# A transformer layer on one core: another prologue order, the loop's pieces and VectorE's order rearranged

## The reference

```python
x = x + attention(layernorm(x))          # eps 1e-5
x = x + ffn(layernorm(x))

def attention(x):                        # 16 heads of 8
    q, k, v = (x @ Wq + bq), (x @ Wk + bk), (x @ Wv + bv)    # then by heads
    q, k, v = (head_layernorm(z, scale, bias) for z in (q, k, v))   # eps 1e-6, over the 8
    scores = einsum('bqhd,bkhd->bhqk', q, k) * 8 ** -0.5
    out = einsum('bhqk,bkhd->bqhd', softmax(scores), v)
    return out.reshape(b, s, 128) @ Wo + bo

def ffn(x):                              # w_gate, w_up (384, 128), w_down (128, 384): int32 / 127
    h = silu(x @ w_gate.T) * (x @ w_up.T)
    return h @ w_down.T
```

## Time and profile before

| | us |
|---|---|
| median of 3 runs | 330.37 (330.34 to 330.46) |
| the profiled execution | 330.57 |
| its span in the trace | 328.8 |
| busy: PE / ACT / DVE / POOL | 297.1 / 268.8 / 238.7 / 48.5 |

### The profile page before, as it was taken

One profiled execution on the slowest core, in us unless ns is written; L12 is line 12 of the kernel. 1 busy time (PEld: TensorE's weight loads), 2 busy tenths in 40 slices (PEclk: granted clock), 3 DMA queues, 4 the chain that ended last, 5 costly groups with the idle time before them and its releaser, 6 DMA issues.

```text
span 328.8 us, 10326 instructions
## 1 busy us (share of the span) xinstructions
PE 297.1 (90%) x4002; PEld 131.8 (40%) x4002; DVE 238.7 (73%) x631; ACT 268.8 (82%) x300; POOL 48.5 (15%) x93
## 2 busy tenths in 40 slices
PE   7877957899999999999999999999998998789996
PEld 7773311233243424352353325342432332222676
DVE  4998997358887797869786888689774856272365
ACT  4429949999989998889979998999889998999511
POOL 7610200041004100140004100410021010110020
PEclk9999989999999999999999999999999999999999
DMA  6534140210325023401422032302320243000000
GB/s 187 161 112 142 34 160 4 80 54 0 101 96 163 2 78 119 139 20 64 127 87 73 0 119 85 116 0 96 96 99 2 66 130 131 2 0 2 34 3 32
DMA packets 21716, 24.76 MB, mean 75 GB/s; under 512 B 2096, under 2 KB 17712, under 8 KB 21680
## 3 DMA queue, kind: packets, MB, share of 16 engines
q1 hardware_dynamic: 21104, 23.59, 22.7%
q10 hardware_dynamic: 576, 0.69, 0.7%
HBM read 15.36 MB, written 8.65 MB: 73 GB/s over the span
## 4 chain that ended last, share of the span: by engine, by line
PE 48%; ACT 26%; issue 13%; DVE 9%; DMA 2%; POOL 1%; ACTq 1%; SPq 0%; POOLq 0%; DVEq 0%
ACT probs L771 25%; PE oacc L912 19%; PE side L844 14%; PE scores L897 9%; PE side L837 3%; DMA y<-in_x 2%; DVE qk_c L1090 1%; PE scores L998 1%; DVE x2n L1074 1%; ACT th L737 1%; PE scores L798 1%; POOL rs L591 1%; PE side L998 1%; DVE stats L1065 0%; DVE sums_t L1256 0%
## 5 line engine op out<-in xcount | busy, mean ns | idle before, releaser
L771 ACT ACTIVATE probs<-scores 128x1536 f32<-128x1536 f32 (+1 forms) x256 | 248.5, 1025 | 31.4 <-PE scores L897 28.3
L912 PE MATMUL oacc<-probs,vaug 128*32 128x512 f32 x1024 | 137.8, 610 | 9.0 <-DVE sums_t L1256 4.0
L897 PE MATMUL scores<-qst,kst 32*128 32x512 f16 x512 | 50.8, 386 | 13.5 <-ACT probs L771 11.2
L897 PEld LDWEIGHTS scores<-qst,kst 32*128 32x128 f16 x512 | 13.0, 91 | 67.7 <-ACT probs L771 58.3
L912 PEld LDWEIGHTS oacc<-probs,vaug 128*32 128x32 f32 x1024 | 20.4, 108 | 42.9 <-ACT probs L771 32.4
L589 POOL TENSOR_SCALAR ve<-mv 128x4 f32<-128x4 f32 (+1 forms) x17 | 4.0, 235 | 222.2 <-DVE mv L1068 190.9
L844 PE MATMUL side<-x2T_parts,gu_parts 128*32 128x512 f16 x504 | 34.9, 379 | 0.8 <-DVE x2T_parts L1296 0.5
L844 PEld LDWEIGHTS side<-x2T_parts,gu_parts 128*32 128x32 f16 x504 | 14.1, 96 | 32.6 <-issue 18.4
L844 PEld LDWEIGHTS side<-wqkv,xT 128*32 128x32 f32 x736 | 20.9, 110 | 12.5 <-issue 11.5
L844 PE MATMUL side<-wqkv,xT 128*32 128x128 f32 x736 | 24.1, 273 | 0.9 <-DMA xT<-in_xT 0.9
L1302 DVE SCALAR_TENSOR_TENSOR ga<-th,side 128x512 f32<-128x512 f32 x21 | 14.4, 685 | 12.1 <-ACT th L737 12.0
(11 more groups left out here) (161 smaller groups left out, 291.0 us busy)
## 6 DMA issues: line engine op xcount, KB each, us to landing
parts_dram<-parts SPq DMA_DIRECT2D x16, 256.0 KB, 2.5
qst<-parts_dram SPq DMA_DIRECT2D x15, 256.0 KB, 2.7
kst<-parts_dram SPq DMA_DIRECT2D x15, 256.0 KB, 3.1
x_res<-in_x SPq DMA_DIRECT2D x8, 256.0 KB, 3.5
parts_dram<-parts SPq DMA_DIRECT2D x16, 128.0 KB, 1.9
x_in<-in_x SPq DMA_DIRECT2D x7, 256.0 KB, 2.6
xT<-in_xT SPq DMA_DIRECT2D x7, 256.0 KB, 3.1
out_dram<-y SPq DMA_DIRECT2D x7, 256.0 KB, 2.1
```

The lines of the kernel that those rows point to most:

```text
L771: act.activation(out, src, ACT.Exp).then_inc(exp_done, 1)
L897: last = pe.matmul(scores[:, j if j < TRIPLE else TRIPLE + u % 2, :], kst[r, g, kt * P:(kt + 1) * P], qst[r, g, :], start=True, stop=True)
L912: last = pe.matmul(oacc[STRIP * j:STRIP * (j + 1), :], vaug[:, kt, NG * g + j, :], probs[:, kt, j, :], start=first, stop=last_of_half)
```

## The change

In the prologue PE makes q's bias alone first and those of k and v between the products of q and k (`BIASES`, `biases`), and ACT copies them in two steps. VectorE does `score_bound` right behind the first statistics, and `ln1_stats(1)`, the second ones, behind `own_parts`; `WARM_FIRST` is 4. In the loop the pieces from `a_rk` to `x2T` stand one unit earlier, unit 7 is empty instead of unit 2, `g2` and `u1` change places, and the banks are dealt anew. VectorE's lists of the first turn and of the others are reordered. No computation is added or left out but the five dummy products.

```diff
-WARM_FIRST = 9
+WARM_FIRST = 4
+BIASES = [slice(3 + ks[0], 4 + ks[-1]) for ks in W_KS]
...
-SIDE = {0: ["a_v"], 1: ["a_rq"], 3: ["a_rk"], 4: ["b_Wo"], 5: ["e_q"], 6: ["e_k"], 7: ["b_x2T"],
-        8: ["b_g0"], 9: ["b_u0"], 10: ["b_g1"], 11: ["b_u1"], 12: ["b_g2"], 13: ["b_u2"], 14: ["b_d0"], 15: ["b_d1"]}
-BANK = {"a_v": 1, "a_rq": 0, "a_rk": 1, "b_Wo": 0, "e_q": 1, "e_k": 0, "b_x2T": 1, "b_g0": 1, "b_u0": 0, "b_g1": 1,
-        "b_g2": 1, "b_u1": 0, "b_u2": 0, "b_d0": 0}
+SIDE = {0: ["a_v"], 1: ["a_rq"], 2: ["a_rk"], 3: ["b_Wo"], 4: ["e_q"], 5: ["e_k"], 6: ["b_x2T"], 8: ["b_g0"],
+        9: ["b_u0"], 10: ["b_g1"], 11: ["b_g2"], 12: ["b_u1"], 13: ["b_u2"], 14: ["b_d0"], 15: ["b_d1"]}
+BANK = {"a_v": 0, "a_rq": 1, "a_rk": 0, "b_Wo": 1, "e_q": 0, "e_k": 1, "b_x2T": 0, "b_g0": 0, "b_u0": 1,
+        "b_g1": 1, "b_g2": 0, "b_u1": 1, "b_u2": 1, "b_d0": 1}
...
-                    if n == 0:
-                        act.wait_ge(b_filled, 1)
-                        act.activation(wqkv[:, 3:6, :], oacc[:, 0:3 * D], ACT.Copy).then_inc(b_centred, 1)
+                    act.wait_ge(b_filled, n + 1)
+                    act.activation(wqkv[:, BIASES[n], :], oacc[:, (BIASES[n].start - 3) * D:(BIASES[n].stop - 3) * D], ACT.Copy)\
+                       .then_inc(b_centred, 1)
...
                     if n == 0:
-                        pe.wait_ge(b_repeated, 1)
-                        for k in range(3):
-                            last = pe.matmul(oacc[:, k * D:(k + 1) * D], b_rep[:, k, :], head_mean_out[:, :],
-                                             start=True, stop=True)
-                        last.then_inc(b_filled, 1)
+                        biases(n)
+
+            def biases(n):
+                pe.wait_ge(b_repeated, 1)
+                at_least(pe, b_centred, n)
+                for k in W_KS[n]:
+                    last = pe.matmul(oacc[:, k * D:(k + 1) * D], b_rep[:, k, :], head_mean_out[:, :], start=True, stop=True)
+                last.then_inc(b_filled, 1)
...
+                if name == "e_k":
+                    biases(1)
                 if name == "a_v":
-                    pe.wait_ge(b_centred, 1)
+                    pe.wait_ge(b_centred, 2)
...
             ln1_stats(0)
-            ln1_stats(1)
             score_bound()
             dve.wait_ge(b_centred, 1)
             centred(0, 0)
+            dve.wait_ge(b_centred, 2)
             centred(0, 1)
...
             own_parts()
+            ln1_stats(1)
             prepare_small()
...
                     centred(2, 1)
+                    take_sums(0, 0)
                     later_square(2, 0)
                     later_square(2, 1)
                     sums_v(1)
-                    take_sums(0, 0)
                     divide(0, 0)
...
-                fill_v(i, 1)
                 if behind:
                     take_sums(i - 1, 1)
+                fill_v(i, 1)
...
                 if ahead:
                     second_part(i + 1)
                 if behind:
                     silu(i - 1, 1, side[:, BANK["b_g1"], :])
                     times_up(i - 1, 1, side[:, BANK["b_u1"], :])
-                if early:
-                    sums_qk(i + 2)
-                if behind:
-                    silu(i - 1, 2, side[:, BANK["b_g2"], :])
-                    times_up(i - 1, 2, side[:, BANK["b_u2"], :])
                 if ahead:
                     if early:
                         dve.wait_ge(hv_done, i + 3)
                     dve.wait_ge(hv_v_done, i + 2)
                     rsqrt_begin(i + 2)
+                if behind:
+                    silu(i - 1, 2, side[:, BANK["b_g2"], :])
+                    times_up(i - 1, 2, side[:, BANK["b_u2"], :])
+                divide(i, 0)
+                if ahead:
                     rsqrt_end(i + 2)
```

More of the change, by code:

```diff
@@ L1398, in turn @@
                     return
-                fill_v(i, 1)
                 if behind:
                     take_sums(i - 1, 1)
+                fill_v(i, 1)
                 if ahead:
                     centred_v(i + 1)
+                if early:
+                    ln1_stats(i + 2)
                 if behind:
                     divide(i - 1, 1)
-                if early:
-                    ln1_stats(i + 2)
+                    turn_heads(i - 1)
                 if ahead:
                     affined(i + 1, 0)
-                if behind:
-                    turn_heads(i - 1)
-                if ahead:
                     affined(i + 1, 1)
@@ L1415, in turn @@
                     ln2_stats(i - 1)
+                if ahead:
+                    sums_v(i + 1)
                 if early:
@@ L1420, in turn @@
                 if early:
+                    later_square(i + 2, 0)
                     centred(i + 2, 1)
@@ L1424, in turn @@
                 take_sums(i, 0)
-                if early:
-                    later_square(i + 2, 0)
                 if ahead:
                     first_part(i + 1)
-                divide(i, 0)
-                if ahead:
-                    sums_v(i + 1)
-                if behind:
-                    silu(i - 1, 0, side[:, BANK["b_g0"], :])
                 if early:
@@ L1436, in turn @@
                 if behind:
+                    silu(i - 1, 0, side[:, BANK["b_g0"], :])
                     times_up(i - 1, 0, side[:, BANK["b_u0"], :])
+                if early:
+                    sums_qk(i + 2)
                 if ahead:
```

## The result

The changed kernel takes 329.59 us (median of 20 runs, 328.18 to 330.58) beside 330.41 for the one before (20 runs): a ratio of 0.9969, 95% interval 0.9956 to 0.9983. It is 0.8 us faster where 4.2 were forecast. The profiled execution has a span of 328.0 against 328.8.

A forecast was written before the change was run, and what follows sets the result against it. The chain of waits (TensorE 48%, ScalarE 26%) was taken to bound the kernel, by whichever of PE and ACT ends last per unit. 330.57 - 3.0 - 1.9 + 0.7 = 326.4, median 326.2 us, range 325.0 to 328.7.

The forecast's parts named there:

- the prologue: Before the first turn: earlier work and the statistics' cost leave a loss of 0.1 us, bounds +1.0 to -0.3.
- the head start of VectorE: Prologue: everything on VectorE up to `own_parts` comes 1.0 us earlier, before the statistics are paid with 1.11 us.
- the first scores come at 23.2: Prologue: with five fewer dummies, 1.2 us less, the first scores start near 23.2.
- First turn, 3.0 us: First turn: `oacc` read out ahead of the squares gains 1.9 us, and 1.1 more as the clock stays up.
- rival 1: First turn: the clock falls although PE's gap is halved, 1.06 us lost, 327.3; chance 0.12.
- The wall at `a_v`: First turn, unit 1: `a_v` waits for VectorE's first four `qk_c`, so the prologue's 1.0 us becomes a longer wait.
- The pieces, 0.27 a turn: Loop: pieces one unit earlier end PE's wait for `x2T_parts`, 0.27 us in each of turns 1 to 7, 1.9 us.
- `d0` late by 0.10: Loop, unit 14: half an rsqrt ahead of the last gate delays `d0` by 0.10 us; 0.7 us lost over six turns.
- Rival 4: Loop: by the semaphore rule `d0` is never late, 325.5; chance 0.07.
- rival 2: Loop: `d0` is late by 0.5 us a turn because late weights do not overlap, 2.4 more, 328.6; chance 0.10.
- the loop's sum: Loop: the sum over the units stays the same as long as each moved piece finds its bank and input ready.

The follow-up runs named there:

- with seven dummies: The kernel with the second statistics behind the bound and the third gate ahead of the rsqrt, with seven dummies instead of ten: 325.47 us, ratio 0.9855.
- the statistics in the gap: The changed kernel with the second statistics between the bound and `qk_c`, and ten dummies instead of four: 326.28 us, ratio 0.9873.
- the kernel with the gate first: The kernel with the statistics in the gap, with the third gate's silu and product moved ahead of the rsqrt's first half: 325.60 us, ratio 0.9858.

## Why the prediction was wrong

**The step that failed: the prologue, "worth -0.1 us", bounds +1.0 and -0.3.** Measured alone it is -3.1 us, ten times the lower bound; in the changed kernel, beside the same kernel without it, -3.8 (329.59 for 325.78). The forecast put the second statistics behind `own_parts` and charged them 1.11 us of VectorE's time and nothing else. It followed VectorE's list and PE's pieces and never looked at who waits for the statistics' counter. That is SyncE's load of x for sequence 2, which nobody needs for a long time, but behind it in the same queue stand the transfers of q's parts, which the first scores need. The rows of before that would have shown it are the queue's: the load of `x_in` at 14.03, ahead of the parts at 19.01. Undoing just this wait brought 2.6 us of the 3.8 back.

**The second part of the same step: PE's pauses were not weighed against the clock.** The statistics also put off `wo`, so PE's bias product comes at 22.24 with a pause of 1.76 us ahead of it (0.64 before), and then the 2.05. I weighed the clock in the first turn and took five dummies away here at full speed. The fall costs 1.2 to 1.6 us at unit 2, as the kernel with twelve dummies shows, and is part of the 2.6. Where the queue is mended, it still comes in one run of five, and costs nothing that the times show.

**A third part, smaller: the head start of VectorE was 0.7 us and not 1.0.** PE's q product ends at 8.63 (forecast 8.5), k's, behind the two bias products, at 10.28 (9.95), and the second four `qk_c` start at 10.41 (10.0), 0.66 ahead of the 11.07 of before; the transposes stand at 16.77 for 17.45. The statistics cost the 1.11 us that were charged, so from `prepare_small` on VectorE is 0.43 later than before (21.76 for 21.33) where the forecast had 0.1. Even with the queue mended the prologue is therefore a loss: 326.98 beside 325.78 without it, 1.2 us, of which the traces show the 0.43 of VectorE and a pause of ACT of 0.35 (below). The rest is within the spread of these runs, and stays open. Nor could the first scores come at 23.2: with seven dummies, in the execution with the earliest start, they wait 0.45 us for k's parts and come at 23.29.

Then the terms that held:
- *First turn, 3.0 us.* Measured alone 3.1. The clock stayed up behind a gap of 1.6, as the 1.53 of the earlier trace rows had suggested; rival 1 is out for this place. In the changed kernel only the place in time was off, by the 2.8 us lost ahead of it. The wall at `a_v` held as well where the statistics stand behind `own_parts`: with the queue mended PE waits 0.69 for `qk_c`, and unit 2 starts at 28.93 for 28.72. With the statistics in the gap the wall itself moves little: `qk_c` is at 25.71 in the kernel with the gate first and at 25.96 in that with the old prologue, unit 2 at 28.23 for 28.29.
- *The pieces, 0.27 a turn.* Units 7 and 8 of turn 3 are 1.94 + 2.13 for 1.95 + 2.40, so 0.28 less, and those of turn 4 0.26 less. But not in seven turns: in turn 1 unit 8 is 0.17 shorter and unit 9 0.16 longer, and the turn gains 0.06 in all; from turn 7 to the end it is 0.12.
- *`d0` late by 0.10.* Unit 14 is 2.89 for 2.80 in turns 2 to 5, and 0.06 longer in turns 1 and 6. With the third gate first again it is back at 2.79 and 2.80, under either prologue. The rule of the Trainium skill (VectorE: DVE Perf Modes, "The DRAIN you can't avoid"), by which a semaphore between two chained operations costs nothing, would have had 0; the 0.78 from the start of silu to that of its product (126.92 to 127.70), for 0.61 to an independent operation (125.06 to 125.67), speaks against it here as well. Rival 4 is out, and rival 2 (0.5 a turn) too.
- *What the loop's sum missed: turn 2.* The forecast took each piece to find its bank ready. In turn 2 `Wo`, now in unit 3, waits for its bank, and ACT is behind by 0.2 (unit 3 is 2.43 for 2.24 in turn 3), because VectorE's four aggregates took 0.84 us there and 0.64 in turn 3. This takes the gain out of turn 2:

```profile
104.17 0.77 DVE L1211 TENSOR_SCALAR qk_f<-side,q_aff 128x512 f32<-128x512 f32 x1
...
104.99 0.81 PEld L848 LDWEIGHTS side<-wo,onT 128*32 128x32 f32 x32 [0.90 <-DVE qk_f L1211]
```

- *A pause of ACT in the first turn.* In the changed kernel and those with its prologue, ACT stops once for 0.41 us at unit 13 and PE behind it for 0.80 (the unit is 2.35 for 2.00), though the scores started no later than in the other units:

```profile
52.71 3.45 ACT L772 ACTIVATE probs<-scores 128x1536 f32<-128x1536 f32 x3 [0.41 <-PE scores L901]
...
54.22 0.40 PE L901 MATMUL scores<-qst,kst 32*128 32x512 f16 x4 [0.80 <-ACT probs L772]
```

These two rows are of the kernel with the gate first. None of the five kernels with the old prologue has it in its trace, all seven with the new one do. The new prologue gives ACT one operation more, the second copy of biases; whether that has to do with it was not tested, and what the pause is stays open. It takes 0.35 of what a mended prologue gains: with seven dummies the first scores are 0.65 earlier than behind the old prologue (23.29 for 23.94), the next turn 0.34 (57.70 for 58.04), and the earlier landing in this one execution is in both.

Without the one wait the kernel comes to 326.98, 0.8 above the forecast of 326.2: VectorE's 0.3, ACT's pause of 0.35, and the loop's gain that was missing, 0.2. That these sum to the difference is no proof of each, since the medians of five runs are only good to some tenths.

## What to carry over

Where an operation is moved back, list everyone who waits for its semaphore, the DMA queues first: a load that nobody needs holds up all that stands behind it in its queue. Price the wait by the transfer behind it that is needed soonest, not by the load itself. And where a change makes several pauses of PE longer, follow the granted clock through each of them before taking dummies away.

## What the runs showed of the hardware

The same kernel has its clock fall for longer in one run than in another, or not at all. In the traces the granted clock is at half for 3.4 us in all where the mean is 0.995 (before, the kernel with the queue mended, that with the old prologue) and for 6.8 us where it is 0.989 or 0.990 (the changed kernel, the loop alone). The changed kernel's 20 runs stand in two groups by this mean: eleven of 0.989 to 0.990 with 329.57 to 330.58 us, nine of 0.994 to 0.995 with 328.18 to 329.28. None has 1.00, so both groups are runs with a fall; by the traces of the other kernels the quicker nine have the shorter one, but none of the nine was traced. The kernel with the old prologue has runs without a fall (1.000 with 325.5 to 325.8) and with one (0.995 with 327.0 to 327.2).

In the traces the pauses behind which the clock stayed up were of 1.53, 1.63, 1.64, 1.66, 1.68, 1.70 and 1.73 us, those behind which it fell of 1.76 (with 2.05 soon after, or in the kernel with the queue mended alone: there the window from 23.5 to 24.0 has 0.61, so the clock falls near 23.6, where the wait of 0.35 only begins), 1.88 and 3.65 to 3.74; but 1.76 left it alone where more dummies followed. The pause itself differs from run to run too: that before the transposes is 1.23, 1.53, 1.68, 1.70 and 1.88 in the five traces of the old prologue, whose code is the same: the inputs land at different times, so the q product starts at 7.18 to 7.83 and the second statistics, which wait for `y`, at 7.21 to 7.56.

What a fall costs depends on what sets the time there. Between the medians of the two groups it is 1.5 us in the kernel with the old prologue, 1.2 where the new prologue stands alone, 1.1 in the changed kernel, 0.5 in the loop alone, and nothing where the queue is mended. The Trainium skill (TensorE: Matmul & The Clock Gate, "Part 1") says that the point of change differs from run to run, of the rise at the start of a kernel; these runs show the like for falls in its middle. One trace is therefore no proof that a pause is harmless.
